# Row maxima of cross attention: the fp32 maxima are transposed, and ScalarE and VectorE form the two bf16 parts behind TensorE

## The reference

```python
x = _layernorm(x + _L0_attn_ref(x, w_project, w_out))         # causal self attention, 16 heads
x = _layernorm(x + _L0_xattn_ref(x, ctx_2048, Wq, ... , bo))  # cross attention, see below
x = _layernorm(x + _L0_ffn_ref(x, w1, b1, ln_g, ln_b, w2, b2))

def _L0_xattn_ref(x, c, Wq, bq, Wk, bk, Wv, bv, Wo, bo):
    # channels are the 64 rows of a batch entry, positions its 256 columns, 8 heads of 8 channels
    q = _apply_rotary(q_emb, split_heads(_proj(x, Wq, bq)))
    k = _apply_rotary(k_emb, split_heads(_proj(c, Wk, bk)))
    v = split_heads(_proj(c, Wv, bv))
    scores = jnp.einsum('bhtc,bhsc->bhts', q, k) / math.sqrt(K_CH)
    p_attn = jax.nn.softmax(scores, axis=-1)
    out = jnp.einsum('bhts,bhsc->bhtc', p_attn, v)
    return _proj(out.transpose(0, 1, 3, 2).reshape(b, 64, t_t), Wo, bo)
```

## Time and profile before

| | us |
|---|---|
| median of 3 runs | 670.93 (668.68 to 674.22) |
| the profiled execution, its own time | 677.3 |
| its span in the trace | 675.4 |

### The profile page before, as it was taken

The page is one execution under the profiler, slowest core; times in us unless marked ns, Lnnn a source line. Parts: engine busy times, 40 slices in busy tenths (PEclk is TensorE's granted clock), DMA queues, the critical chain, the costliest instruction groups (busy, mean ns, idle before and its releaser), DMA issues. The chain is left out here.

```text
span 675.4 us, 12183 instructions
## 1 busy us (share of the span) xinstructions
PE 490.2 (73%) x3986; PEld 253.3 (38%) x4002; DVE 522.3 (77%) x1045; ACT 378.3 (56%) x681; POOL 319.9 (47%) x383
## 2 busy tenths in 40 slices
PE   5556888889888888898898888788966414545445
PEld 3332435444444344444443444333222103333333
DVE  6476678978988879889888898778437677888885
ACT  1211346555556555555565656477548958677673
POOL 6442435364464553644645537320020057776773
PEclk9787779999999999999999999878567955555555
DMA  7212522212222223132222221220000000000000
GB/s 260 59 43 74 177 67 65 68 51 74 75 65 62 64 68 83 49 76 69 72 60 66 66 77 49 51 71 4 1 0 1 0 0 8 16 16 23 16 17 32
DMA packets 51400, 37.04 MB, mean 55 GB/s; under 512 B 21392, under 2 KB 47376, under 8 KB 51216
## 3 DMA queue, kind: packets, MB, share of 16 engines
q1 hardware_dynamic: 51344, 36.33, 18.8%
HBM read 24.52 MB, written 10.49 MB: 52 GB/s over the span
## 5 line engine op out<-in xcount | busy, mean ns | idle before, releaser
L729 ACT ACTIVATE PB<-e_b 128x512 f32<-128x512 f32 x256 | 149.5, 594 | 115.7 <-PE e_b L559 115.3
L907 DVE TENSOR_REDUCE MX<-mx_b 128x2 f32<-128x512 f32 x256 | 171.4, 681 | 44.0 <-PE mx_b L531 43.2
L531 PE MATMUL mx_b<-KA,QA 48*128 48x256 bf16 x512 | 101.3, 287 | 15.0 <-DMA QA<-parts_q 8.4
L559 PE MATMUL e_b<-QA,KA 50*128 50x256 bf16 x512 | 99.5, 289 | 9.6 <-DMA QA<-MR 7.4
L574 PE MATMUL u_b<-PB,VA 128*32 128x256 f32 x1024 | 88.7, 420 | 4.2 <-ACT PB L729 4.1
L823 POOL TENSOR_TENSOR SP<-SP,srec 128x1024 f32<-128x1024 f32 x14 | 26.6, 1901 | 101.4 <-DVE srec L864 101.4
L531 PEld LDWEIGHTS mx_b<-KA,QA 48*128 48x128 bf16 x512 | 31.5, 96 | 96.3 <-DVE MX L907 41.9
L1325 PE MATMUL r_b<-att_tab,Q 128*128 128x128 f32 x128 | 31.5, 427 | 37.5 <-ACT Q L1249 37.4
L818 POOL TENSOR_TENSOR KM<-QK,att_tab 128x1024 f32<-128x1024 f32 x30 | 57.0, 1904 | 1.6 <-ACT QK L684 1.6
L1317 PE MATMUL z_b<-w2q,Q2T 128*128 128x256 bf16 x128 | 30.2, 417 | 37.0 <-ACT Q2T L1272 26.3
L295 POOL TENSOR_TENSOR rs<-mv,epsc 128x1 f32<-128x1 f32 x32 | 6.1, 190 | 96.2 <-DVE mv L283 66.6
(11 more groups left out here) (197 smaller groups left out, 1125.4 us busy)
## 6 DMA issues: line engine op xcount, KB each, us to landing
KA<-parts_k SPq DMA_DIRECT2D x64, 96.0 KB
QA<-parts_q SPq DMA_DIRECT2D x64, 96.0 KB
parts_q<-part_q SPq DMA_DIRECT2D x32, 128.0 KB, 1.9
parts_k<-part_k SPq DMA_DIRECT2D x16, 192.0 KB, 2.1
XT<-in_xT SPq DMA_DIRECT2D x16, 128.0 KB, 2.4
X<-in_x SPq DMA_DIRECT2D x16, 128.0 KB, 2.2
C<-in_ctx SPq DMA_DIRECT2D x16, 128.0 KB, 2.1
out_y<-O SPq DMA_DIRECT2D x16, 128.0 KB, 1.7
```

Source lines behind the costliest of these rows:

```text
L531: m = nc.tensor.matmul(mx_b[n % 2][:, D * k:D * k + D], QA[low:low + K_MAX, 2 * i.ring + b, h, P * u:P * u + P], KA[low:low + K_MAX, 2 * i ...
L559: m = nc.tensor.matmul(e_b[n % 2][:, D * k:D * k + D], KA[low:low + K_EXP, 2 * i.ring + b, h, P * sc:P * sc + P], QA[low:low + K_EXP, 2 * ...
L729: nc.scalar.activation(PB[:, n % 4].rearrange("p e t -> p (e t)"), e_b[n % 2][:, :], ACT.Exp, scale=XC ** -0.5).then_inc(e_sb.sem, 1)
L907: nc.vector.tensor_reduce(MX[:, b, e, 2 * q:2 * q + 2, u], mx_b[n % 2][:, :].rearrange("p (e s) -> p e s", e=2), AXL.X, ALU.max).then_inc( ...
```

## The change

`negate` and the tile NM are gone. PE multiplies MX itself (128x16, fp32, as weights) by the fp32 identity and so has the transposed maxima, 16x128, in g_b[1]. ACT writes their negative, rounded to bf16, to MR[0:16]. DVE gets a new step, `mt_low`, that reads the bank once more and writes the remainder to MR[32:48]; it waits for ACT's copy. It stands in slot 4 (b = 1 of pair i) and slot 13 (b = 0 of pair i+1), behind the slot's max tile, and in slot 13 ahead of `minus_max`. The event mt_sb now counts 4 a pair, and both SP's DMAs and PE's next use of g_b[1] wait for `mt_low`. A max tile that overwrites MX waits for PE's transpose, not for `negate`. The two DMAs carry one part each (high, low) in place of one half each.

```diff
-        NM = sb("NM", [P, 2, 2, 8], BF16)
-        MR = sb("MR", [32, P], BF16)
+        MR = sb("MR", [64, P], BF16)
...
-        mx_ps, mx_red, negm = event("mx_ps", 16), event("mx_red", 16), event("negm", 4)
-        mt_ps, mt_sb = event("mt_ps", 2), event("mt_sb", 2)
+        mx_ps, mx_red = event("mx_ps", 16), event("mx_red", 16)
+        mt_ps, mt_sb = event("mt_ps", 2), event("mt_sb", 4)
...
             def max_rows(i, b):
-                wait(sp, mt_sb, i, b + 1)
-                for e in range(2):
-                    low = HALF * e + ROW_M
-                    sp.dma_start(QA[low:low + 2, 2 * i.ring + b].rearrange("m h (u t) -> m (h u) t", u=2),
-                                 MR[16 * e:16 * e + 16, :]).then_inc(mrow[i.ring][b], 16)
+                wait(sp, mt_sb, i, 2 * b + 2)
+                for m in range(2):
+                    sp.dma_start(QA[ROW_M + m:ROW_M + m + HALF + 1:HALF, 2 * i.ring + b].rearrange("e h (u t) -> e (h u) t", u=2),
+                                 MR[32 * m:32 * m + 16, :]).then_inc(mrow[i.ring][b], 16)
...
             def max_transpose(i, b, g):
-                ps = use(g_b[g], mt_sb, i, b + 1)
-                wait(pe, negm, i, 2 * b + 2)
-                nc.tensor.transpose(ps[0:32, 0:64].bitcast(BF16), NM[:].rearrange("p e m c -> p (e m c)"),
-                                    identb[:]).then_inc(mt_ps.sem, 1)
+                ps = use(g_b[g], mt_sb, i, 2 * b + 2)
+                wait(pe, mx_red, i, 8 * b + 8)
+                nc.tensor.matmul(ps[0:16, 0:P], MX[:, b].rearrange("p e h u -> p (e h u)"), ident,
+                                 start=True, stop=True).then_inc(mt_ps.sem, 1)
...
-                nc.scalar.activation(MR[:, :], g_b[g][0:32, 0:64].bitcast(BF16), ACT.Copy).then_inc(mt_sb.sem, 1)
+
+                nc.scalar.activation(MR[0:16, :], g_b[g][0:16, 0:P], ACT.Copy, scale=-1.0).then_inc(mt_sb.sem, 1)
...
                 if n % 8 == 0 and has(i, 1):
-                    wait(dve, negm, i.plus(-1), 2 * b + 2)
+                    wait(dve, mt_ps, i.plus(-1), b + 1)
...
-            def negate(i, b):
-
-                wait(dve, mx_red, i, 8 * b + 8)
-                if b == 1:
-                    wait(dve, mt_ps, i, 1)
-                elif has(i, 1):
-                    wait(dve, mt_ps, i.plus(-1), 2)
-                nc.vector.tensor_scalar(NM[:, :, 0, :], MX[:, b].rearrange("p e h u -> p e (h u)"), -1.0, None, ALU.mult).then_inc(negm.sem, 1)
-                wait(dve, negm, i, 2 * b + 1)
-                nc.vector.scalar_tensor_tensor(out=NM[:, :, 1, :], in0=MX[:, b].rearrange("p e h u -> p e (h u)"), scalar=-1.0, in1=NM[:, :, 0, :],
-                                               op0=ALU.mult, op1=ALU.subtract).then_inc(negm.sem, 1)
+            def mt_low(i, b, g):
+                wait(dve, mt_sb, i, 2 * b + 1)
+                nc.vector.scalar_tensor_tensor(out=MR[32:48, :], in0=g_b[g][0:16, 0:P], scalar=-1.0, in1=MR[0:16, :],
+                                               op0=ALU.mult, op1=ALU.subtract).then_inc(mt_sb.sem, 1)
...
             for n in range(8):
                 max_tile(p0, n)
-            negate(p0, 0)
+            mt_low(p0, 0, 1)
...
                         max_tile(nxt, n)
-                        if n % 8 == 7:
-                            negate(nxt, n // 8)
...
                     if s == 2 and rotary:
                         rotate("k", g_b[0], j)
+                    if s == 4:
+                        mt_low(i, 1, 1)
+                    if s == 13 and not last:
+                        mt_low(i.plus(1), 0, 1)
```

## The result

The changed kernel takes 691.19 us (median of 4, 688.83 to 695.41), the kernel before in the same runs 671.39 (668.68 to 674.22): the ratio is 1.030, 95% interval 1.024 to 1.037. It is slower by 19.8 us; the forecast was 12.1 slower. The profiled execution took 690.47 us with a span of 688.7, only 13.2 us over the profiled one of before.

The account below looks back on a forecast made before the run. The prediction took the order of handovers between PE and DVE as the bound. 13 x 0.9 = 11.7 us plus 0.6 for body 13 gave +12.3 profiled, put as 670.9 + 12.1 = 683.0 us; range 674 to 695.

Parts of the forecast that it names:

- `negate` goes: Removing `negate` in slot 9 starts the rotation of q 0.30 us earlier a body, on both ways round the loop.
- The 1.2 us of slot 1: `negate` holds DVE 1.2 us in slot 1; at most 0.3 reaches the following reductions, and 0.1 was taken.
- `mt_low`'s price: The new DVE step's own duration, put at 0.29 us, with bounds 0.17 and 0.43.
- Slot 4: The transposes wait for `mt_low` behind a reduction and start 0.89 us later: +0.9 a body, bounds 0.57 to 1.13.
- Slot 13: PE's L458 and the scores wait for `mt_low` behind a reduction: +1.4 us a body, bounds 1.3 to 1.55.
- The DMA waits that were to swallow 1.14 of it: PE's waits in slots 0 (0.53) and 2 (0.61) absorb 1.14 us a body of the delay in slot 13.
- The body: Phase A's body grows by 0.86 us, +0.9 with up to 0.1 for matmuls not hidden, to 27.7 us.
- the term: Bodies 0 to 12 have both waits: 13 x 0.9 = 11.7 us.
- The step that failed: Behind body 12: body 13 has transposes but no scores, +0.6 us; bodies 14 and 15 have neither, 0.
- The clock's: Rival, chance 0.07: PE's longer gaps in slots 4 and 13 drop TensorE to its lower clock, up to 705 us.
- DVE is relieved: Rival, chance 0.07: DVE is the bound and loses work, a body gains 0.9 us, the whole takes 658 us.
- swallowed: Rival, chance 0.14: the waits are mostly absorbed, a body costs about +0.35 us, the whole +5: 676 us.

Follow-up runs that it names:

- no_low_slot4: The changed kernel with `mt_low` left out in slot 4, so the low part of b = 1 sent is an older one: 679.9 us.
- no_low_slot13: The changed kernel with `mt_low` left out in slot 13 (b = 0) and kept in slot 4: 677.8 us.
- after_again: The changed kernel itself, profiled and timed once more: 693.3 us, ratio 1.032 to the kernel before.
- twice: The changed kernel with each `mt_low` done two times, the extra one into an unused tile: 697.2 us.
- five: The changed kernel with each `mt_low` done 5 times, the four extra ones into an unused tile: 732.2 us.
- early: The changed kernel with `mt_low` ahead of the max tile of slots 4 and 13 in place of behind it: 677.3 us.
- no_low: The changed kernel with `mt_low` left out in both slots and the low row sent as zero: 664.2 us, ratio 0.989 to the kernel before.
- high_only: The changed kernel without `mt_low` and without the low row: one DMA of maxima, 49 rows in place of 50: 663.1 us.
- wait_slot4: The kernel before plus a small DVE step in slot 4 only, which reads g_b[1] and which PE's next use of the bank waits for: 692.5 us.
- wait_alone: The kernel before plus a small DVE step in slots 4 and 13, which reads g_b[1] and which PE's next use of the bank waits for: 722.9 us.

## Why the prediction was right, and where it was off

The direction, the range and the mechanism held; the size was 12.1 for 19.8 us.

**`negate` goes.** In slot 9 the rotation of q is earlier: from the transposes L474 (298.58 in the body that the earlier trace rows belong to) to it were 10.9 us, from L472 at 306.63 to 317.13 are 10.5: 0.4 where 0.30 was put. The 1.2 us of slot 1 gave little, as said: rot_k now starts 0.04 us after PE's L507, and the reductions behind it wait for PE.

**`mt_low`'s price** was put at 0.29 and measured 0.28 in all 32 cases (line L912 among those of tile MR, in ns). In 14 of them, those of slot 4, POOL was at work beside it, and it took no longer. L918 before, which read and wrote SBUF, took 0.17 to 1.43 us. This agrees with the Trainium skill, "SBUF — State Buffer", section "SBUF: two separate sides", as the prediction used it for an operand in PSUM.

```profile
L912 DVE SCALAR_TENSOR_TENSOR MR<-g_b,MR x32: 280/280/281, 66.7 to 497.1; 16x128 bf16<-16x128 f32 x32
```

**Slot 4.** +0.9 was forecast. From k's projection L508 to the transposes were 2.98 us (322.56 to 325.54), now 306.63 - 302.77 = 3.86: +0.88. no_low_slot4 gives it back, 0.88.

**Slot 13.** +1.4 was forecast. From the rotation of q to L458 were 3.89 us, now 322.35 - 317.13 = 5.22: +1.33. The DMA waits that were to swallow 1.14 of it did go, from 13.1 us to 0.8; by no_low_slot13, 0.58 of the step was exposed.

**The body**: +0.86 to +0.9 by the sum; 28.12 - 27.08 = +1.04. So it was sized a little short. From body 0 to 13 the two kernels' profiles took 356.1 and 352.0 before, 366.3 and 366.0 after: +12.1 on average, where 11.7 was the term. That part was right, with help from the slow body 0 of the first profile of before: 13 bodies of 1.04 would be 13.5.

**The step that failed** is the last one of the sum: "Body 13 has transposes but no scores: +0.6. Bodies 14 and 15 have neither ...: 0." From body 13 to the feed-forward it is 67.7 and 68.9 after, 65.2 and 61.2 before: +5.1 on average where +0.6 was put. By bodies it is +2.4 in body 13, +2.8 in body 14 and -0.1 behind. Two waits in there I had missed, both in this timeline of after:

```profile
464.75 0.59 PE L581 MATMUL g_b<-wsum,ones 128*128 128x2 f32 x2 [1.09 <-DVE MR L912]
...
489.50 1.03 SPq L358 DMA_DIRECT2D QA<-MR  x2
...
491.67 0.28 PE L557 MATMUL e_b<-QA,KA 50*128 50x256 bf16 x1 [1.14 <-DMA QA<-MR]
```

In body 13 the next user of g_b[1] in slot 13 is the weight sum's matmul, L581, and waits as the scores do. In body 14 SP has no store of q ahead of the maxima, so that they leave the moment `mt_low` is done (489.47), and the short body leaves PE waiting 1.14 us for them. With slot 4 of body 13 (0.7 more of waiting) that is 2.9 us. The rest goes with the clock, and for body 14 the runs show whose it is. With the low part in slot 13 and SP waiting for it, body 14, measured as above, took 22.6 and 23.2 us (after, after_again), 23.1 (twice), 23.8 (five), 22.1 (no_low_slot4) and 21.0 (early, where the step comes sooner). Without it, it took 19.1 (no_low_slot13) and 19.0 (no_low, high_only). PEclk in it was 0.65 in the two profiles after, 0.75 and 0.76 before, 0.80 in no_low_slot13. So where it stands behind a reduction the step of slot 13 costs 3 to 4 us there, more than the 1.14 us of waiting, and the clock goes down with it. Body 14 in after, then in no_low_slot13:

```profile
474.16 0.27 ACT L722 ACTIVATE MR<-g_b 16x128 bf16<-16x128 f32 x1
...
496.80 0.27 ACT L722 ACTIVATE MR<-g_b 16x128 bf16<-16x128 f32 x1
```

```profile
467.13 0.27 ACT L722 ACTIVATE MR<-g_b 16x128 bf16<-16x128 f32 x1
...
486.27 0.25 ACT L722 ACTIVATE MR<-g_b 16x128 bf16<-16x128 f32 x1
```

What stands behind body 14 took 19.9 and 16.4 us before, 17.6 and 18.6 after; there, and in body 13, chance and the change are not told apart.

Over both profiles of each kernel the spans are 17.4 us apart: 12.1 from body 0 to 13, 5.1 behind, 0.2 ahead. The medians' 19.8 are 2.4 more, which no trace locates. The first profile of before, from which the sum started, was 6 us over its median, while the one after was at its own. That the two profiled executions lie only 13.2 us apart, near the 12.3 of the sum, was luck.

**The rivals.** The clock's had 0.07 and did not come in bodies 1 to 11 of this kernel, whose gap in slot 4 is 1.19. It was near: in wait_slot4 a gap of 1.51 was once followed by a fall; of the gaps of 2.0 in the ten bodies, five of ten were in five and nine of nine in wait_alone, at 1.5 us a body in five. And in body 14, where the prediction had put nothing, PEclk was 0.65 in place of 0.75. "DVE is relieved" and "swallowed" did not come.

## What to carry to other kernels

A bank shared by small jobs makes its slowest reader the gate of an in-order engine: when a second reader is added behind the first, price what stands ahead of that reader in its own queue (here reductions of 0.7 us each), not only its 0.28 us. If the step must be there, put it ahead of the engine's next long job; two moved lines gave back 14 of 20 us, and leaving the low part out, which a softmax that divides by its own sum allows, beat the kernel before by 1.1%.
Read a stretch that differs from the steady loop by itself, and profile twice before two profiled executions are subtracted.

## What the runs showed of the hardware

- TensorE's granted clock fell behind an idle gap of 1.97 us in five of ten bodies of one execution (five) and not behind the same gap in the other five. In wait_slot4 it fell behind gaps of 1.51, 1.69 and 1.74 us and not behind 1.72 and 1.83. With gaps of 1.38 (twice) and 1.19 (after) in that place, bodies 1 to 11 stayed at 1.00. A fall cost 1.5 us a body in five.
- A DVE instruction of 0.28 us added only 0.19 us when a like one stood ahead of it without a wait between (twice).
- An fp32 matmul with 16 columns of weights stands in the records as two matmuls of 0.27 to 0.28 us, 0.12 us apart (after); in no_low, whose body is shorter than before, its cost does not show.
